# Adapter probabilities and values appended to each head's own 64 keys: transposes of 74 columns and value matmuls of 74 rows in four column tiles

## The chip, the cores and the metric

The kernel runs on one core of one Trainium2 chip. The metric is the device time of one execution in microseconds (us); lower is better. The time before is the median of three runs.

## What is computed

Two layers on `x` of shape (32, 64, 1024), kept in float32:

1. `x = x + attn(cond(x))`: a conditioned 64x64 mixing of channels, then causal self-attention with 32 heads of width 32, rotary angles, and an adapter: 10 learned prefix tokens whose keys and values come from the same weights.
2. `x = x + ffn(cond2(x))`: a grouped convolution, a 1024x1024 linear layer and a routed low-rank addition.

The change is in the attention only. The lines that matter there:

```python
attn = softmax(where(causal, q @ k.T / sqrt(hd), -inf))     # 64 keys per sequence
y = attn @ v
ascores = gating[0] * softmax(q @ ak.T / sqrt(C))           # 10 adapter keys, a softmax of its own
y = y + ascores @ av
out = y @ w_proj
```

The two softmaxes are separate, but both products end in the same `y`.

## The kernel before

Engines are programmed by hand, each with its own list of instructions and semaphores. The attention is 8 groups of 4 heads (`g`, 128 channels each) times 4 units of 512 tokens (`u`): 32 units `n = 4 g + u`. A unit has 8 sequences of 64 tokens, that is 4 pairs `s` of two (`b`).

On TensorE a unit (`unit_step`, L977) runs in this order: scores of the unit before (L900, four row tiles by two column tiles, one bank `bS[h]` for each head, a slot of 74 columns: 64 own keys and 10 adapter keys), transposes of its values (L960), projection of K (24 matmuls, L948), of Q (24), in a group's first unit the adapter's keys and values (`project_adapter`, L972, 16 starts in four column tiles), then the transposes of the probabilities of the unit before (`attend_transposes`, L906), projection of V (24), and last the value matmuls of the unit before (`attend_values`, L920). In a group's first unit `turn_adapter` (L936) stands in the middle of V. After unit 31 the same steps stand between the first products of the projection layer.

The softmax of a unit is on VectorE (`attend_softmax`, L1382) with exponentials on ScalarE (`attend_exp`, L1173). The own probabilities lie in `prob[t]`, two heads in each half of the columns, so that one transpose turns 2 x 64 columns. The adapter probabilities are weighted by the gate, split into a high part, a low part and the high part again (L1425 to L1428), and written as 3 x 40 columns of `aprob`; four transposes turn them (L909). ScalarE copies the turned banks back (`attend_copies`, L1180: `aT` and two `pT`). The adapter's product is then one reduced-precision matmul per unit over all four heads, with a block-diagonal `avbd` that VectorE prepares per group from two parts (L1648 to L1653); the own products add to it, with a block-diagonal `vbd` for two heads at once:

```python
pe.matmul(y[:], avbd[:], aT[:], start=True, stop=True)                               # L925
for s, b, hp:                                                                        # 16 matmuls
    pe.matmul(y[64*hp : 64*hp+64, cols], vbd[:, s, b, hp, :], pT[hp][:, s, 64*b:...]) # L931
```

A float32 matmul that is not a transpose appears in the trace as two starts, so L931 has 32 in a unit and L900 64. ScalarE fills `vbd` with four copies (L1291). SP stores the finished `y` and moves the prepared weights of the second layer (`store_prep`, L691) and, in a group's last unit, the next group's weights `w_st` (L754); `split_hi` (L1165) on ScalarE waits for these. After the attention come eight groups of projection products (L1026) and eight of the second layer (convolution L1044, products L1026, low rank L1078).

Of the kernel before, what the change touches and what calls it, by code (L numbers as in the profile page):

```python
# [32 lines left out]
P = 128  # L33
# [348 lines left out]
def program(nc, d, psum, z, zbase, y_dram, x1_dram, w_forms, ctx_dram, aggb_dram, weights, out):  # L382
# [8 lines left out]
    with ExitStack() as ctx:  # L391
# [64 lines left out]
        aprob = sb("aprob", [P, UP, P], F32R)  # L456
        atmp = sb("atmp", [P, UP * GH, NA])
        astat = sb("astat", [P, 3, UP * GH])
        aT = sb("aT", [P, UT], F32R)
        akv = sb("akv", [AC * AP_, 2 * P])  # L460
        avbd = sb("avbd", [P, P], F32R)
        avs = sb("avs", [P, P])
        avh = sb("avh", [P, P], F32R)
        asel = sb("asel", [AC * AP_, P])
        afold = sb("afold", [AC * AP_, NA])
        alow = sb("alow", [P, 1])
        amask = sb("amask", [P, P])
# [24 lines left out]
        bAT, bPT, bAD = bS[0], bS[1:3], bS[3]  # L492
        score_slots = psum[:, 0:GH * UP * SW].rearrange("p (h s c) -> p h s c", h=GH, c=SW)
        AKT, AVS = 2 * P, 3 * P
        AR = GH * NA
# [29 lines left out]
        agated = sem("a_agated")  # L525
        aprobs = sem("a_aprobs")
        a_tr = sem("a_a_tr")
        aT_copied = sem("a_aT_copied")
# [3 lines left out]
        avh_set = sem("a_avh_set")  # L532
        aweighted = sem("a_aweighted")
        aprob_hi = sem("a_aprob_hi")
# [6 lines left out]
        NCONST, NCLEAR, NFCONST = 10, 3, 3  # L541
# [48 lines left out]
        def place(t):  # L590
# [7 lines left out]
            (place(kbd_pad), place(qr), place(bbase), [place(t) for t in (x8[0], prob[0], pT[0], vbd)],  # L598
             [place(t) for t in (vT, aprob, aT, ysb)], attn.at))
        mix_sync, mix_clear, mix_tensor, mix_scalar, mix_vector = parts  # L600

        block = ctx.enter_context(nc.Block())

# [6 lines left out]
        def refill(g, u):  # L610

            return u == NU - 1 and not last(g)

# [46 lines left out]
        def _(sp):  # L660
            mix_sync.begin(sp)
            for dst, src in ((wte[:, 0:KC * NA], "wteT"), (cosT[:], "cos"), (sinT[:], "sin"), (mask[:], "mask"), (ident[:], "ident"),
                             (gate[:], "gate"), (asel[:], "asel"), (amask[:], "amask"), (afold[:], "afold"), (alow[:], "alow")):
                sp.dma_start(dst, d[src]).then_inc(consts, 16)
# [190 lines left out]
        def _(pool):  # L855
            mix_clear(pool)
            pool.memset(wte[:, KC * NA:], 0.0).then_inc(cleared, 1)
            pool.wait_ge(z_sum, 2 * UP)
            pool.memset(aprob[:].bitcast(F32), 0.0).then_inc(cleared, 1)
            pool.wait_ge(z_mm, NP)  # L860
            pool.memset(vbd[:], 0.0).then_inc(cleared, 1)
# [23 lines left out]
        def _(pe):  # L885
            mix_tensor.begin(pe)
            def attend_scores(m, groups):
# [48 lines left out]
            def turn_adapter(g):  # L936
                pe.wait_ge(akv_copied, g + 1)
                pe.matmul(bAD[:, AVS:AVS + P], asel[:], akv[:, P:2 * P], start=True, stop=True)
                pe.matmul(bAD[:, AKT:AKT + NA], akv[:, 0:P], afold[:], start=True, stop=True).then_inc(ak_tr, 1)
# [23 lines left out]
            def project_adapter(g, n):  # L963
# [5 lines left out]
                wait(pe, ashifted, n)  # L969
                for c in range(KC):  # L970
                    part = c % AP_
                    mm = pe.matmul(bAD[AC * part:AC * (part + 1), 0:2 * P], wte[:, c * NA:c * NA + AC],  # L972
# [141 lines left out]
            pe.wait_ge(ashifted, NG * NU)  # L1114
# [39 lines left out]
        def _(act):  # L1154
# [18 lines left out]
            def attend_exp(m):  # L1173
                for t in range(2):
                    act.wait_ge(shifted, 2 * m + t + 1)
                    act.activation(prob[t][:], prob[t][:], ACT.Exp, scale=SCALE).then_inc(exped, 1)  # L1176
                act.wait_ge(ashifted, m + 1)
                act.activation(atmp[:], atmp[:], ACT.Exp, scale=ASCALE).then_inc(aexped, 1)
# [65 lines left out]
            def unit_step(g, u):  # L1244
# [42 lines left out]
                if n == 0:  # L1287
                    act.wait_ge(cleared, NCLEAR)
# [561 lines left out]
```

## Time and profile before

| | |
|---|---|
| median of 3 runs | 1140.98 us (1140.66 to 1142.0) |
| span of the profiled execution, first to last instruction | 1139.1 us |
| its own time as a run | not listed apart; the median lies 1.9 us above its span |
| TensorE busy | 1132.2 us, 99% |
| VectorE busy | 923.4 us, 81% |
| ScalarE busy | 359.6 us, 32% |
| GpSimd busy | 54.1 us, 5% |
| granted TensorE clock, mean over the span | 1.000 |

In the profile a matmul's duration reaches from its start to the modelled end of its result, so matmuls in a row overlap; what one costs is read from start to start. Rows of the timeline merge instructions of one kind that follow each other: a start, the length of the whole piece, and their count.

### The profile page before, as it was taken

To read this page: it belongs to the slowest core of one execution; us is meant where nothing else is said; L and a number is where in the kernel's file an instruction comes from. 1 tells how busy PE (TensorE), PEld (TensorE's weight loads), DVE (VectorE), ACT (ScalarE), POOL (GpSimd) and SP (SyncE) were. 2 spreads that over 40 slices of the span, in tenths; PEclk is the share of its full clock that TensorE was granted. 3 is DMA by queue.
4 is the path that set the end of the run, shared out by engine and by line. 5 is a ranking of instruction groups with operands and counts; after the bars stand their busy time and mean duration, and the time that the engine had idled before them with its cause. 6 is when DMAs were issued, how large, how long until landed. Compare 5 with 4: busy or idle time off the path is not lost.

```text
span 1139.1 us, 21477 instructions
## 1 busy us (share of the span) xinstructions
PE 1132.2 (99%) x8632; PEld 950.7 (83%) x8632; DVE 923.4 (81%) x1740; ACT 359.6 (32%) x665; POOL 54.1 (5%) x24
## 2 busy tenths in 40 slices
PE   9999999999999999999999999999999999999998
PEld 6888888888888888888888888878888888888887
DVE  5999879879889789798798799888767777877765
ACT  5433333333342432433433334323222211122210
POOL 0000000000000000000000000110000022221112
PEclk9999999999999999999999999999999999999999
DMA  6515115114125034034033177885549933233312
GB/s 222 182 56 167 67 34 162 66 53 153 56 75 167 20 97 155 12 106 146 20 111 130 45 270 269 322 251 164 185 129 347 345 89 104 96 116 116 98 38 93
DMA packets 99701, 151.81 MB, mean 133 GB/s; under 512 B 7443, under 2 KB 84115, under 8 KB 96915
## 3 DMA queue, kind: packets, MB, share of 16 engines
q1 hardware_dynamic: 98594, 135.76, 36.5%
q10 hardware_dynamic: 1008, 14.68, 3.1%
q8 instruction: 69, 1.13, 0.4%
q14 instruction: 30, 0.24, 0.1%
HBM read 95.88 MB, written 54.54 MB: 132 GB/s over the span
## 4 chain that ended last, share of the span: by engine, by line
PE 92%; DVE 4%; DMA 2%; issue 1%; ACT 0%; SPq 0%; DVEq 0%; ACTq 0%
PE psum L948 44%; PE psum L1026 23%; PE psum L1044 5%; PE psum L931 3%; PE psum L916 2%; PE psum L900 2%; PE psum L1078 2%; PE psum L1060 2%; PE psum L276 2%; DMA y_scratch<-a_ysb 2%; PE psum L960 2%; PE psum L909 1%; PE psum L1062 1%; PE psum L972 1%; PE psum L230 1%
## 5 line engine op out<-in xcount | busy, mean ns | idle before, releaser
L948 PE MATMUL psum<-z,w_hi 128*128 128x512 f32 x1536 | 481.5, 395 | 0.2 <-DVE z L374 0.2
L948 PEld LDWEIGHTS psum<-z,w_hi 128*128 128x128 f32 x1536 | 282.5, 188 | 57.2 <-DVE z L374 0.4
L948 PE MATMUL psum<-z,w_lo 128*128 128x512 f32 x768 | 300.5, 391 | 0.0
L1026 PE MATMUL psum<-f_wform,f_act_hi 128*128 128x512 f32 (+1 forms) x912 | 279.9, 389 | 1.3 <-DVE f_u L1494 1.1
L1026 PEld LDWEIGHTS psum<-f_wform,f_act_hi 128*128 128x128 f32 x912 | 167.9, 188 | 35.8 <-issue 2.6
L1026 PE MATMUL psum<-f_wform,f_act_lo 128*128 128x512 f32 (+1 forms) x456 | 176.2, 386 | 0.0
L948 PEld LDWEIGHTS psum<-z,w_lo 128*128 128x128 f32 x768 | 144.1, 188 | 30.6
L1026 PEld LDWEIGHTS psum<-f_wform,f_act_lo 128*128 128x128 f32 x456 | 85.7, 188 | 17.4
L875 POOL TENSOR_TENSOR f_xn<-f_x,_bbase 128x1024 f32<-128x1024 f32 x16 | 50.5, 3158 | 1009.0 <-DVE f_x L1520 678.5
L1218 ACT ACTIVATE f_act_hi<-f_act_sum 128x512 fp32r<-128x512 f32 x64 | 40.3, 632 | 119.2 <-DVE f_act_sum L1469 48.1
L1218 ACT ACTIVATE f_act_hi<-f_raw 128x512 fp32r<-128x512 f32 x56 | 33.7, 626 | 102.7 <-DVE f_raw L1552 64.8
L1394 DVE TENSOR_TENSOR a_prob<-psum,a_mask 128x512 f32<-128x512 f32 x64 | 43.9, 687 | 26.4 <-PE psum L900 26.3
L1475 DVE TENSOR_TENSOR f_act_lo<-f_act_sum,f_act_hi 128x512 fp32r<-128x512 f32 x64 | 48.6, 762 | 16.5 <-ACT f_act_hi L1218 16.5
L1475 DVE TENSOR_TENSOR f_act_lo<-f_raw,f_act_hi 128x512 fp32r<-128x512 f32 x56 | 37.2, 689 | 28.6 <-ACT f_act_hi L1218 28.5
L1183 ACT ACTIVATE a_aT<-psum 128x512 fp32r<-128x512 f32 x32 | 19.2, 599 | 122.0 <-PE psum L909 121.8
L1291 ACT ACTIVATE a_vbd<-psum 64x256 f32<-64x256 f32 x128 | 48.5, 379 | 26.3 <-PE psum L960 25.1
L1176 ACT ACTIVATE a_prob<-a_prob 128x512 f32<-128x512 f32 x64 | 40.5, 633 | 51.4 <-DVE a_prob L1399 50.9
L1372 DVE STREAM_SHUFFLE a_rot<-psum 128x512 f32<-128x512 f32 x64 | 47.2, 737 | 0.0
L1411 DVE TENSOR_TENSOR a_prob<-a_prob,a_stat 128x512 f32<-128x512 f32 x64 | 44.3, 692 | 2.2
L1375 DVE TENSOR_TENSOR a_rot<-a_rot,a_sin 128x512 f32<-128x512 f32 x64 | 44.3, 692 | 2.2
L1399 DVE TENSOR_TENSOR a_prob<-a_prob,a_stat 128x512 f32<-128x512 f32 x64 | 44.3, 692 | 2.2
L1397 DVE TENSOR_REDUCE a_stat<-a_prob 128x8 f32<-128x512 f32 x64 | 44.0, 687 | 2.2
(173 smaller groups left out, 1491.7 us busy)
## 6 DMA issues: line engine op xcount, KB each, us to landing
w_forms<-f_prep_lo SPq DMA_DIRECT2D x16, 896.0 KB, 5.2
f_wform<-w_forms SPq DMA_DIRECT2D x7, 2048.0 KB, 13.2
f_wform<-w_forms ACTq DMA_DIRECT2D x7, 2048.0 KB, 16.9
w_st<-in_wqkvT SPq DMA_DIRECT2D x7, 1536.0 KB, 6.3
w_forms<-f_prep_hi SPq DMA_DIRECT2D x16, 640.0 KB, 6.2
m_x<-in_x SPq DMA_DIRECT2D x16, 512.0 KB, 5.5
y_scratch<-a_ysb SPq DMA_DIRECT2D x32, 256.0 KB, 2.8
f_raw<-y_scratch SPq DMA_DIRECT2D x8, 1024.0 KB, 6.0
```

What stands on the lines that cost most here:

```text
L875: pool.tensor_tensor(xn[:, t, :].rearrange("p (m q) -> p q m", q=PH), x1[:, t, :].rearrange("p (q m) -> p q m", q=PH), bbase[:].rearrange( ...
L948: mm = pe.matmul(dst, w[:, c, x, :], zs, start=(c == 0 and i == 0), stop=(c == KC - 1 and i == 2))
L1026: mm = pe.matmul((prod_bank[i], bank[0])[part][:, cols], a[:, c, :], wform[i][:, w, c, cols], start=(i < 4 and c == 0 and n == 0), stop=(c ...
L1044: mm = pe.matmul(conv_banks(p)[:, o:o + P], x8[p % 2][:, CONV * b + g, j:j + P], toep[:, g, j, :], start=(j == 0), stop=(j == 1))
L1218: act.activation(act_hi[f][:], src, ACT.Copy).then_inc(act_hi_set, 1)
L1291: cp = act.activation(vbd[NC * h:NC * (h + 1), :, b, :, HD * h:HD * (h + 1)], bV[NC * b:NC * (b + 1), :].rearrange("p (s a h e) -> p s a h ...
L1372: dve.stream_shuffle(rot[:], src[:], HALF_SWAP).then_inc(turned[x], 1)
L1375: dve.tensor_tensor(r, r, tab[1], ALU.mult).then_inc(rot_step, 1)
L1397: dve.tensor_reduce(stat[:, t, 0, :], prob[t][:], AX, ALU.max).then_inc(row_max, 1)
L1399: dve.tensor_tensor(prob[t][:], prob[t][:], spread(t, 0), ALU.subtract).then_inc(shifted, 1)
L1411: dve.tensor_tensor(prob[t][:], prob[t][:], spread(t, 2), ALU.mult).then_inc(probs, 1)
L1475: dve.tensor_tensor(act_lo[f][:], src, act_hi[f][:].bitcast(F32), ALU.subtract).then_inc(act_set, 1)
```

## The change

Each head gets its own strip of 74 columns in `prob`, 64 own probabilities and behind them its 10 adapter probabilities. A transpose turns 128 tokens x 74 columns (16 in a unit, into the four score banks), ScalarE copies 74 rows four times, and the value matmul of a head has 74 rows: the keys' values (`vkeys`, rows 0 to 63) and the adapter's values times the gate (rows 64 to 73, copied per group from `avt`). The four heads go to four column tiles of 32. The separate adapter matmul, its split into parts, `aprob`, `aT`, `avbd`, `avs`, `avh`, two constants (`amask`, `alow`, two DMAs on SP's queue) and two clearing writes on GpSimd are gone. From group 1 on the adapter's projection stands in the bank of `y` and no longer in `bS[3]`.

```diff
-        vbd = sb("vbd", [P, UP, 2, 2, 2 * HD])
-        prob = [sb(f"prob{t}", [P, 8, NC]) for t in range(2)]
-        pT = [sb(f"pT{t}", [P, UP, P]) for t in range(2)]
+        vkeys = sb("vkeys", [P, UP, 2, P])
+        prob = sb("prob", [P, GH, UP, KW])
+        pT = sb("pT", [P, GH, UT])
...
             def attend_scores(m, groups):
-                wait(pe, aT_copied, m)
-                wait(pe, pT_copied, 2 * m)
-                wait(pe, ashifted, m)
+                wait(pe, pT_copied, GH * m)
...
             def attend_transposes(m):
-                pe.wait_ge(aprobs, 2 * m + 2)
-                for i in range(UP):
-                    tr = pe.transpose(bAT[:, i * P:(i + 1) * P], aprob[:, i, :].bitcast(F32),
-                                      ident[:])
-                tr.then_inc(a_tr, 1)
-                wait(pe, pT_copied, 2 * m)
-                for t, dst in enumerate(bPT):
-                    pe.wait_ge(probs, 2 * m + t + 1)
-                    for j in range(4):
-                        tr = pe.transpose(dst[:, j * P:(j + 1) * P],
-                                          prob[t][:, 2 * j:2 * j + 2, :].rearrange("p h k -> p (h k)"), ident[:])
+                pe.wait_ge(aprobs, m + 1)
+                for h in range(GH):
+                    pe.wait_ge(probs, 2 * m + h // 2 + 1)
+                    for s in range(UP):
+                        tr = pe.transpose(bS[h][0:KW, s * P:(s + 1) * P], prob[:, h, s, :], ident[:])
                     tr.then_inc(p_tr, 1)
 
             def attend_values(m, groups):
                 y = y_bank(m)
-                pe.wait_ge(aT_copied, m + 1)
+                turns = min((m + 1) // NU + 1, NG)
+                pe.wait_ge(akbd_set, turns)
+                pe.wait_ge(avs_set, turns)
                 pe.wait_ge(avbd_set, groups)
                 wait(pe, y_copied, m)
-                pe.matmul(y[:], avbd[:], aT[:], start=True, stop=True)
                 pe.wait_ge(vbd_set, m + 1)
-                pe.wait_ge(pT_copied, 2 * m + 2)
+                pe.wait_ge(pT_copied, GH * (m + 1))
                 for s in range(UP):
                     for b in range(2):
-                        for hp in range(2):
-                            mm = pe.matmul(y[2 * HD * hp:2 * HD * (hp + 1), (2 * s + b) * NC:(2 * s + b + 1) * NC],
-                                           vbd[:, s, b, hp, :], pT[hp][:, s, NC * b:NC * b + NC],
-                                           start=False, stop=True, skip_group_check=True)
+                        for h in range(GH):
+                            rows = slice(HD * h, HD * (h + 1))
+                            cols = slice((2 * s + b) * NC, (2 * s + b + 1) * NC)
+                            mm = pe.matmul(y[rows, cols], vkeys[0:KW, s, b, rows], pT[0:KW, h, cols], start=True, stop=True)
...
             def attend_copies(m):
-                act.wait_ge(a_tr, m + 1)
                 wait(act, y_mm, m)
-                act.activation(aT[:], bAT[:], ACT.Copy).then_inc(aT_copied, 1)
-                for t, src in enumerate(bPT):
-                    act.wait_ge(p_tr, 2 * m + t + 1)
-                    act.activation(pT[t][:].rearrange("p s q -> p (s q)"), src[:], ACT.Copy).then_inc(pT_copied, 1)
+                if m == 0:
+                    act.wait_ge(z_sum, 3 * UP)
+                for h in range(GH):
+                    act.wait_ge(p_tr, GH * m + h + 1)
+                    act.activation(pT[0:KW, h, :], bS[h][0:KW, :], ACT.Copy).then_inc(pT_copied, 1)
...
-                dve.tensor_scalar(astat[:, 2, :], astat[:, 2, :], gate[:, 0:1], None, ALU.mult).then_inc(agated, 1)
-                dve.tensor_tensor(atmp[:], atmp[:], aspread(2), ALU.mult).then_inc(aweighted, 1)
-                dve.tensor_copy(parts[:, 0], flat).then_inc(aprob_hi, 1)
-                dve.tensor_tensor(parts[:, 1], flat, parts[:, 0].bitcast(F32), ALU.subtract).then_inc(aprobs, 1)
-                dve.tensor_copy(parts[:, 2], parts[:, 0].bitcast(F32)).then_inc(aprobs, 1)
+                dve.tensor_tensor(prefix, prefix, aspread(2), ALU.mult).then_inc(aprobs, 1)
```

Three places in the order of the instructions. First, TensorE between the end of Q's projection (`z`, `w_hi`, `w_lo`: activations and weights in parts) and V's, in the second unit; `_ident` is the moving identity. Before, and then with the change:

```order
L948 MATMUL psum<-z,w_hi 128x512 x2
L948 MATMUL psum<-z,w_lo 128x512
L909 MATMUL psum<-_ident,a_aprob 128x128 x4
L916 MATMUL psum<-_ident,a_prob_107 128x128 x4
L916 MATMUL psum<-_ident,a_prob_108 128x128 x4
```

```order
L931 MATMUL psum<-z,w_hi 128x512 x2
L931 MATMUL psum<-z,w_lo 128x512
L898 MATMUL psum<-_ident,a_prob 74x128 x16
L931 MATMUL psum<-z,w_hi 128x512 x2
L931 MATMUL psum<-z,w_lo 128x512
```

Twelve transposes of 128x128 have become sixteen of 74x128; line numbers moved with the file (L948 is now L931).

Second, TensorE behind V's projection, where the value matmuls stand. Before (the pair of `a_pT` rows comes eight times in all), and then with the change:

```order
L948 MATMUL psum<-z,w_hi 128x512 x2
L948 MATMUL psum<-z,w_lo 128x512
L925 MATMUL psum<-a_aT,a_avbd 128x512
L931 MATMUL psum<-a_pT_109,a_vbd 64x64
L931 MATMUL psum<-a_pT_110,a_vbd 64x64
```

```order
L931 MATMUL psum<-z,w_hi 128x512 x2
L931 MATMUL psum<-z,w_lo 128x512
L915 MATMUL psum<-a_pT,a_vkeys 32x64 x32
L887 MATMUL psum<-a_kbd,a_qr 64x74 x32
L943 MATMUL psum<-_ident,a_vT 128x128 x4
```

The matmul of 512 columns is gone, sixteen matmuls of 64x64 have become thirty-two of 32x64, and scores (now L887) and value transposes (now L943) follow as they did.

Third, VectorE at the end of a softmax, where the adapter's part stands ahead of the rotation of K (`a_kr`). Before, and then with the change:

```order
L1413 TENSOR_REDUCE a_astat<-a_atmp 128x16
L1415 RECIPROCAL a_astat<-a_astat 128x16
L1417 TENSOR_SCALAR a_astat<-a_astat,a_gate 128x16
L1420 TENSOR_TENSOR a_atmp<-a_atmp,a_astat 128x160
L1425 CAST a_aprob<-a_atmp 128x4x4x10
L1427 TENSOR_TENSOR a_aprob<-a_atmp,a_aprob 128x4x4x10
L1428 CAST a_aprob<-a_aprob 128x4x4x10
L1370 TENSOR_TENSOR a_kr<-psum,a_cos 128x512
```

```order
L1392 TENSOR_TENSOR a_prob<-a_prob,a_stat 128x8x64
L1394 TENSOR_REDUCE a_astat<-a_prob 128x16
L1396 RECIPROCAL a_astat<-a_astat 128x16
L1398 TENSOR_TENSOR a_prob<-a_prob,a_astat 128x16x10
L1352 TENSOR_TENSOR a_kr<-psum,a_cos 128x512
```

Four of the seven adapter steps are gone, and the rotation of K follows the weighting directly.

## Rows read from the trace of the kernel before

**Rows 1.** The page: busy time and share of each engine, and TensorE's granted clock by slices.

```profile
PE 1132.2 (99%) x8632; PEld 950.7 (83%) x8632; DVE 923.4 (81%) x1740; ACT 359.6 (32%) x665; POOL 54.1 (5%) x24
...
PEclk9999999999999999999999999999999999999999
```

**Rows 2.** Waits of TensorE, longest of eight: us in total, times, longest.

```profile
PE psum L230 <- DVE m_busy L319: 1.5, 1, 1.5
```

**Rows 3.** Timeline of TensorE, one unit: start us, us, line, tiles, shapes, count.

```profile
327.87 0.60 PE L909 MATMUL psum<-_ident,a_aprob 128*128 128x128 f32 x4
328.31 1.04 PE L916 MATMUL psum<-_ident,a_prob 128*128 128x128 f32 x8
329.10 0.71 PE L948 MATMUL psum<-z,w_hi 128*128 128x512 f32 x2
...
334.44 0.39 PE L948 MATMUL psum<-z,w_lo 128*128 128x512 f32 x1
334.67 0.39 PE L925 MATMUL psum<-a_aT,a_avbd 128*128 128x512 f32 x1
334.99 1.15 PE L931 MATMUL psum<-a_pT,a_vbd 128*64 128x64 f32 x32
336.07 0.94 PE L900 MATMUL psum<-a_kbd,a_qr 32*64 32x74 f32 x64
336.94 0.66 PE L960 MATMUL psum<-_ident,a_vT 128*128 128x128 f32 x4
```

**Rows 4.** Groups of TensorE weight loads by form: busy us, mean ns.

```profile
L1044 PEld LDWEIGHTS psum<-_toep,_x 128*128 128x128 f32 x256 | 29.3, 192 | 0.1
L916 PEld LDWEIGHTS psum<-_ident,a_prob 128*128 128x128 f32 x256 | 28.9, 140 | 0.0
```

**Rows 5.** Groups of TensorE matmuls by form: busy us, mean ns.

```profile
L1044 PE MATMUL psum<-_toep,_x 128*128 128x128 f32 x256 | 29.9, 275 | 0.0
L972 PE MATMUL psum<-w_st,a_wte 128*32 128x256 f32 x128 | 8.6, 385 | 0.0
```

**Rows 6.** Timeline of TensorE at the adapter's projection in a group's first unit.

```profile
305.81 1.07 PE L972 MATMUL psum<-w_st,a_wte 128*32 128x256 f32 x16
306.81 0.66 PE L909 MATMUL psum<-_ident,a_aprob 128*128 128x128 f32 x4
```

**Rows 7.** Timeline of VectorE at the end of a softmax, same unit as rows 3.

```profile
324.96 0.23 DVE L1417 TENSOR_SCALAR a_astat<-a_astat,a_gate 128x16 f32<-128x16 f32 x1
325.23 0.32 DVE L1420 TENSOR_TENSOR a_atmp<-a_atmp,a_astat 128x160 f32<-128x160 f32 x1
325.59 0.24 DVE L1425 CAST a_aprob<-a_atmp 128x160 fp32r<-128x160 f32 x1
...
326.12 0.23 DVE L1428 CAST a_aprob<-a_aprob 128x160 fp32r<-128x160 f32 x1
```

**Rows 8.** Timeline of ScalarE in the last unit of group 1.

```profile
205.87 1.06 ACT L1171 ACTIVATE w_hi<-w_st 128x1024 fp32r<-128x1024 f32 x1 [10.57 <-DMA w_st<-in_wqkvT]
206.95 0.60 ACT L1183 ACTIVATE a_aT<-psum 128x512 fp32r<-128x512 f32 x1
207.45 1.08 ACT L1186 ACTIVATE a_pT<-psum 128x512 f32<-128x512 f32 x2
208.40 1.07 ACT L1171 ACTIVATE w_hi<-w_st 128x1024 fp32r<-128x1024 f32 x1
```

**Rows 9.** Timeline of TensorE in the same unit.

```profile
208.29 0.39 PE L925 MATMUL psum<-a_aT,a_avbd 128*128 128x512 f32 x1
208.68 1.15 PE L931 MATMUL psum<-a_pT,a_vbd 128*64 128x64 f32 x32
```

**Rows 10.** Waits of SP's queue, that for the second layer's stored weights.

```profile
SPq L753 <- DMA w_forms<-a_prep_hi_two: 30.7, 7, 4.7
```

**Rows 11.** Timeline of VectorE in group 3's first unit.

```profile
311.76 0.29 DVE L1648 TENSOR_TENSOR a_avs<-psum,a_amask 128x128 f32<-128x128 f32 x1 [1.23 <-ACT a_kbd L1267]
```

**Rows 12.** Timeline of TensorE in the same unit.

```profile
314.17 0.39 PE L925 MATMUL psum<-a_aT,a_avbd 128*128 128x512 f32 x1
```

More of the change, by code:

```diff
@@ L540, in program @@
         y_out = sem("a_y_out")
-        NCONST, NCLEAR, NFCONST = 10, 3, 3
+        NCONST, NFCONST = 8, 3
         fconsts = sem("f_consts")
@@ L597, in program, with own @@
             (wst, whi, wlo, whi_f, w_first, w_hi, w_lo),
-            (place(kbd_pad), place(qr), place(bbase), [place(t) for t in (x8[0], prob[0], pT[0], vbd)],
-             [place(t) for t in (vT, aprob, aT, ysb)], attn.at))
+            (place(kbd_pad), place(qr), place(bbase), [place(t) for t in (x8[0], prob, pT, vkeys)],
+             [place(vT), place(pT) + 2 * UT * 4, place(pT) + 3 * UT * 4, place(ysb)], attn.at))
         mix_sync, mix_clear, mix_tensor, mix_scalar, mix_vector = parts
         block = ctx.enter_context(nc.Block())
+        prefix = prob[:].rearrange("p h s c -> p (h s) c")[:, :, NC:KW]
+        def own(t):
+            return prob[:, 2 * t:2 * t + 2, :, 0:NC].rearrange("p h s k -> p (h s) k")
         def first(g, u):
@@ L612, in refill, with adapter_bank @@
             return u == NU - 1 and not last(g)
+        def adapter_bank(g):
+            return bY if g else bS[3]
         def y_bank(m):
@@ L968, in project_adapter @@
                 pe.wait_ge(w_lo[V_], g + 1)
-                wait(pe, ashifted, n)
+                wait(pe, y_copied, n - 1)
                 for c in range(KC):
                     part = c % AP_
-                    mm = pe.matmul(bAD[AC * part:AC * (part + 1), 0:2 * P], wte[:, c * NA:c * NA + AC],
+                    mm = pe.matmul(adapter_bank(g)[AC * part:AC * (part + 1), 0:2 * P], wte[:, c * NA:c * NA + AC],
                                    wst[:, c, K_:V_ + 1, :].rearrange("p x c -> p (x c)"),
@@ L1286, in unit_step @@
                 wait(act, y_mm, n)
-                if n == 0:
-                    act.wait_ge(cleared, NCLEAR)
-                for b in range(2):
-                    for h in range(2):
-                        cp = act.activation(
-                            vbd[NC * h:NC * (h + 1), :, b, :, HD * h:HD * (h + 1)],
-                            bV[NC * b:NC * (b + 1), :].rearrange("p (s a h e) -> p s a h e", s=UP, a=2, h=2)[:, :, :, h, :],
-                            ACT.Copy)
+                if u == 0:
+                    act.wait_ge(avs_set, g + 1)
+                    act.activation(vkeys[NC:KW, :, :, :].rearrange("p s b f -> p (s b) f"),
+                                   avt[NC:KW, :].rearrange("p (a f) -> p a f", a=1).broadcast_to([NA, UB, P]),
+                                   ACT.Copy).then_inc(avbd_set, 1)
+                for b in range(2):
+                    cp = act.activation(vkeys[0:NC, :, b, :], bV[NC * b:NC * (b + 1), :].rearrange("p (s f) -> p s f", s=UP),
+                                        ACT.Copy)
                 cp.then_inc(vbd_set, 1)
@@ L1392, in attend_softmax @@
                     dve.wait_ge(scores, 2 * m + t + 1)
-                    wait(dve, p_tr, 2 * m)
-                    dve.tensor_tensor(prob[t][:].rearrange("p (s h) k -> p h s k", h=2),
-                                      score_slots[:, 2 * t:2 * t + 2, :, 0:NC], maskb, ALU.add).then_inc(masked, 1)
+                    wait(dve, p_tr, GH * m)
+                    dve.tensor_tensor(prob[:, 2 * t:2 * t + 2, :, 0:NC], score_slots[:, 2 * t:2 * t + 2, :, 0:NC], maskb, ALU.add
+                                      ).then_inc(masked, 1)
                     dve.wait_ge(masked, 2 * m + t + 1)
-                    dve.tensor_reduce(stat[:, t, 0, :], prob[t][:], AX, ALU.max).then_inc(row_max, 1)
+                    dve.tensor_reduce(stat[:, t, 0, :], own(t), AX, ALU.max).then_inc(row_max, 1)
                     dve.wait_ge(row_max, 2 * m + t + 1)
-                    dve.tensor_tensor(prob[t][:], prob[t][:], spread(t, 0), ALU.subtract).then_inc(shifted, 1)
+                    dve.tensor_tensor(own(t), own(t), spread(t, 0), ALU.subtract).then_inc(shifted, 1)
                 asrc = score_slots.rearrange("p h s c -> p (h s) c")[:, :, NC:KW]
@@ L1402, in attend_softmax @@
                 dve.wait_ge(amax, m + 1)
-                wait(dve, aprobs, 2 * m)
-                dve.tensor_tensor(atmp[:], asrc, aspread(0), ALU.subtract).then_inc(ashifted, 1)
+                dve.tensor_tensor(prefix, asrc, aspread(0), ALU.subtract).then_inc(ashifted, 1)
                 for t in range(2):
                     dve.wait_ge(exped, 2 * m + t + 1)
-                    dve.tensor_reduce(stat[:, t, 1, :], prob[t][:], AX, ALU.add).then_inc(row_sum, 1)
+                    dve.tensor_reduce(stat[:, t, 1, :], own(t), AX, ALU.add).then_inc(row_sum, 1)
                     dve.wait_ge(row_sum, 2 * m + t + 1)
@@ L1410, in attend_softmax @@
                     dve.wait_ge(inverted, 2 * m + t + 1)
-                    dve.tensor_tensor(prob[t][:], prob[t][:], spread(t, 2), ALU.mult).then_inc(probs, 1)
+                    dve.tensor_tensor(own(t), own(t), spread(t, 2), ALU.mult).then_inc(probs, 1)
                 dve.wait_ge(aexped, m + 1)
-                dve.tensor_reduce(astat[:, 1, :], atmp[:], AX, ALU.add).then_inc(asum, 1)
+                dve.tensor_reduce(astat[:, 1, :], prefix, AX, ALU.add).then_inc(asum, 1)
                 dve.wait_ge(asum, m + 1)
@@ L1647, in unit_step @@
                     wait(dve, avbd_set, g)
[L1648 to L1653 removed]
+                    dve.tensor_scalar(avt[NC:KW, :], adapter_bank(g)[NC:KW, AVS:AVS + P], gate[NC:KW, 0:1], None, ALU.mult
+                                      ).then_inc(avs_set, 1)
                 if n == 0:
@@ L1783, in constants @@
     q, k = np.arange(P)[:, None] % NC, np.arange(NC)[None, :]
-    row, part = np.arange(P) % (GH * NA), np.arange(P) // (GH * NA)
     kv = np.arange(AC * AP_) % AC
     return {
-        "asel": ((row[None, :] % NA == kv[:, None]) & (part < 3)[None, :]).astype(np.float32),
+        "asel": ((kv[:, None] < NA) & (np.arange(P)[None, :] - NC == kv[:, None])).astype(np.float32),
         "afold": (kv[:, None] == np.arange(NA)[None, :]).astype(np.float32),
-        "alow": (part == 2)[:, None].astype(np.float32),
-        "amask": ((row[:, None] // NA == np.arange(P)[None, :] // HD) & (part < 3)[:, None]).astype(np.float32),
         "cos": np.tile(np.concatenate([cos, cos], 0), (GH, 1)),
```

51 lines of the change are left out of this document (9 added, 42 removed).

## The prediction

> **What bounds the kernel now.** First the page [rows 1]: TensorE is busy 1132.2 of 1139.1 us, 99%, and its clock is granted in full in all forty slices. VectorE stands at 81%, ScalarE at 32%. A busy TensorE need not be a bound, since durations overlap, so the next view is the list of its waits: there are eight in the whole span, the longest 1.5 us at the very start, before the attention [rows 2]. In the attention TensorE waits for nobody. So an instruction that it is given more, or spared, moves the end by its own start-to-start cost, and what VectorE or ScalarE save is worth nothing by itself. The third view is therefore TensorE's timeline of one unit [rows 3], where costs are read as the distance from one start to the next. All that the change does to the time is in two places of that unit, 32 times.
>
> **Transposes: 12 become 16.** Four transposes take 328.31 - 327.87 = 0.44 us, 0.11 us each [rows 3]. The question is what that price hangs on, because a transpose now has 74 columns in its stationary operand and still streams the 128 columns of the identity. The rows let the two be told apart: the load of a transpose takes 140 ns and that of a full float32 matmul 192 ns [rows 4], yet a 128-column float32 start of the convolution has nearly the same busy time per start, 29.9 us over 256 starts or 0.117 us [rows 5], as the transposes' 0.11. A load shorter by 52 ns bought almost nothing. I take the streamed 128 columns as the price, unchanged: 16 x 0.11 instead of 12 x 0.11, +0.44 us a unit. The other end, a price that falls with the columns, is the first rival.
>
> **The adapter's own matmul goes.** From the last start of V at 334.44 to L925 at 334.67 is 0.23 us, and L925 is an ordinary 512-column start in that row of starts [rows 3]. Without it the value matmuls follow V directly; the change of tiling in front of them stands either way. So -0.23 us a unit.
>
> **Value matmuls: 32 starts in two column tiles become 64 in four.** Before, the block takes 336.07 - 334.99 = 1.08 us [rows 3]. No row shows the new form, so I bound it. What a streamed column costs: 385 ns for 256 columns against 275 ns for 128 [rows 5], 110 ns per 128, so 0.055 us for 64. With two tiles at once 32 starts are 16 rounds, 0.88 us, and 0.20 us of the 1.08 are entry, exit and loads. With four tiles at once 64 starts are again 16 rounds, 0.88 us. That four tiles of 128 rows by 32 columns do run at once is what the adapter's projection shows: 16 starts of 256 columns take 306.81 - 305.81 = 1.00 us [rows 6]; four at once is 4 x 0.22 = 0.88 us plus 0.12, two at once would be 1.76. So the block is 1.00 us if its remainder is the projection's 0.12, and 1.08 if it is the old block's 0.20. A high bound comes from charging the projection's 0.12 us in full to its four rounds, 0.03 a round: 16 x 0.085 = 1.36 us. The old block, with 16 rounds as well, is the nearest row and contradicts that (0.20 in 16 rounds), so I take 1.05, -0.03 us a unit; 1.00 and 1.36 stay as ends.
>
> **ScalarE.** Three copies of turned banks become four. In the tightest place they run 207.45 - 206.95 = 0.50 us apart [rows 8], so the last ends 0.5 us later, beside V's projection (334.44 - 329.10 = 5.3 us [rows 3]). Only in the last unit of a group is that cover thin, because the copies stand behind a weight copy that waited 10.57 us for the DMA [rows 8]; in group 1 they end at 207.45 + 1.08 = 208.53 and the value matmuls start at 208.68 [rows 9]. If that cover went, 0.5 us less the 0.18 us by which the values start later would be exposed, 0.3 us, in seven units at most: 2 us. But it should widen: VectorE's adapter tail loses 325.23 - 324.96 = 0.27 us and 326.12 + 0.23 - 325.59 = 0.76 us, some 1.0 us [rows 7]; the prepared weights that VectorE makes in a group's third unit are then stored earlier, and SP waits for that store (seven times, up to 4.7 us [rows 10]) before it asks for the next weights. The four copies into `vbd` become two of twice the size, and per group ten rows are copied once more; ScalarE has room for both.
>
> **VectorE, SP, GpSimd.** The softmax ends 1.0 us earlier than 326.35 and the transposes it feeds start at 327.87 [rows 3, 7]: slack becomes more slack. In a group's first unit the values now also wait for the adapter's values, set at 311.76 + 0.29 = 312.05 [rows 11]; L925 stood at 314.17 there [rows 12], so 2 us are left. SP's queue has two constants fewer to send in the first stage and GpSimd two clears fewer; nothing that TensorE waits for is among them, so zero.
>
> **The sum.** +0.44 - 0.23 - 0.03 = +0.18 us a unit, 32 units, +5.8 us. Against the profiled execution: span 1139.1 becomes 1144.9; the median of the runs lies 1.9 us above that span and I leave that distance, so 1141.0 + 5.8 = **1146.8 us**, 0.5% slower. With the low end of the block: +0.13 a unit, +4.2, 1145.2. With the high end: +0.49 a unit, +15.7, 1156.7, of little weight for the reason given.
>
> **Rival 1, faster: the transpose's price follows its 74 columns.** Place: the 16 transposes of a unit. If a start cost 74/128 of 0.11, 0.064 us, they would take 1.02 instead of 1.32 us, and the unit 0.30 + 0.23 + 0.03 = 0.56 us less: -17.9 us, 1123.1. The point at which it decides is a price of (1.32 + 0.26)/16 = 0.099 us: below it the kernel gets faster. For it: the stationary operand really is narrower. Against it: the comparison of loads above [rows 4, 5]. I give 0.06 to a clear gain and another 0.06 to a price near 0.099, which would be no change. The Trainium skill, "TensorE: Matmul & The Clock Gate", section "LDWEIGHTS (loading the stationary operand)", says that a load's time goes by its columns, 1/1.2 ns each; by that rule the loads of 74 columns get shorter, and this rival follows if loads set the pace. The rows show that transposes' loads are not what sets it.
>
> **Rival 2, much slower: only two tiles at once.** If 64 starts ran in pairs, the block would be 32 x 0.055 + 0.20 = 1.96 us, +0.88: the unit +1.09, +34.9 us, 1175.9. Against it: the projection's 1.00 us [rows 6]. What could still part the two is 74 rows instead of 128. Chance 0.04.
>
> **Rival 3, much slower: a price per start.** The old block spends 1.08/32 = 0.034 us on a start; 64 starts at that price are 2.16 us, +1.08, the unit +1.29, +41.3 us, 1182.3. Against it stand the scores, 64 starts in 336.94 - 336.07 = 0.87 us, 0.0136 each [rows 3], and the new block needs only 0.0164. Chance 0.04. The Trainium skill has such a rule on the same page, in the section "Wait — 56ns, not 53.3ns?": starts never come closer than about 25 ns, however few columns. By it the block would take at least 64 x 0.025 = 1.6 us, an estimate of 1164 us for the run; this trace's scores disagree with it by almost a factor of two, since they run on several tiles.
>
> **Rival 4, a little more: thin covers.** The late copies above are exposed after all, or the scores behind the longer block start with fewer instructions ready. Up to 2 us for the first; the second I bound by 0.05 us a unit, the difference between 1.05 and the block's 1.00, 1.6 us. That is 1147 to 1150.4, the same sign. Chance 0.08.
>
> **How the numbers follow.** The forecast gets 0.72, and with rival 4 the band from 1145.2 to 1150.4 holds 0.80. The low end of the range goes a step towards rival 1, to a transpose of 0.105 us: 16 x 0.105 - 1.32 - 0.26 = +0.10 us a unit, +3.2, 1144.2. The high end stays at 1150.4. About 0.2%, or 2.3 us, is what a measurement of this kernel tells from no change: under 1138.7 faster, above 1143.3 slower. Faster 0.06 (rival 1), same 0.06, slower 0.88 (0.72 + 0.08 + 0.04 + 0.04).
>
> **What would show it.** Right: sixteen transposes whose starts stay 0.11 us apart, about 1.75 us to V's first start; V's last start followed directly by the value matmuls; 64 of these in 1.0 to 1.1 us up to the first score; the scores' 0.87 us kept; no new waits of TensorE. Wrong: transposes closer than 0.10 us (rival 1); starts of value matmuls coming two at a time, or evenly 0.03 us apart (rivals 2 and 3); waits of the value matmuls for `a_pT` in each group's last unit (rival 4). If the time fell while TensorE's timeline showed these costs, the claim that nothing else bounds the kernel would be wrong.

## The result, and the profile after

| | before | after |
|---|---|---|
| median of 7 runs each, us | 1142.0 (1140.66 to 1144.9) | 1148.02 (1144.92 to 1152.8) |
| ratio of the times | | 1.0059, 95% interval [1.0047, 1.0071] |
| span of the profiled execution, us | 1139.1 | 1143.1 |

The changed kernel is slower by 0.6%, about 6 us. Its profiled execution took 1144.92 us, the fastest of its seven runs; why will be seen below. The page after, busy time of each engine and granted clock, against [rows 1]:

```profile
PE 1134.9 (99%) x9752; PEld 954.4 (83%) x9752; DVE 891.9 (78%) x1596; ACT 372.0 (33%) x641; POOL 52.8 (5%) x22
...
PEclk9999999999999999999999999999999999999999
```

VectorE lost 31.5 us of work and TensorE won nothing by it. VectorE's timeline shows where the softmax now ends:

```profile
325.80 0.33 DVE L1398 TENSOR_TENSOR a_prob<-a_prob,a_astat 128x160 f32<-128x160 f32 x1
```

It ends at 326.13 and the transposes start at 328.72, 2.59 us later, where 1.52 us lay between them before [rows 3, 7]: slack became more slack. TensorE's timeline of the unit that [rows 3] show (start us, us, line, tiles, shapes, count):

```profile
328.49 0.39 PE L931 MATMUL psum<-z,w_lo 128*128 128x512 f32 x1
328.72 1.91 PE L898 MATMUL psum<-_ident,a_prob 128*74 128x128 f32 x16
330.38 0.71 PE L931 MATMUL psum<-z,w_hi 128*128 128x512 f32 x2
...
335.72 0.39 PE L931 MATMUL psum<-z,w_lo 128*128 128x512 f32 x1
336.04 1.10 PE L915 MATMUL psum<-a_pT,a_vkeys 74*32 74x64 f32 x64
337.07 0.94 PE L887 MATMUL psum<-a_kbd,a_qr 32*64 32x74 f32 x64
337.95 0.66 PE L943 MATMUL psum<-_ident,a_vT 128*128 128x128 f32 x4
```

Read from start to start:

| step of a unit, us | before [rows 3] | after | difference |
|---|---|---|---|
| transposes, to V's first start | 329.10 - 327.87 = 1.23 | 330.38 - 328.72 = 1.66 | +0.43 |
| V's last start to the first value matmul | 334.99 - 334.44 = 0.55 | 336.04 - 335.72 = 0.32 | -0.23 |
| value matmuls, to the first score | 336.07 - 334.99 = 1.08 | 337.07 - 336.04 = 1.03 | -0.05 |
| scores, to the transposes of the values | 0.87 | 0.88 | +0.01 |

That is +0.16 us a unit. The view of one line gives the first and last start of its instructions; the scores' line spans units 0 to 31, so 31 units from first to last (fields after the count: shortest, median and longest ns, then first to last start). Before, after, and the changed kernel profiled a second time:

```profile
L900 PE MATMUL psum<-a_kbd,a_qr x2048: 222/223/273, 64.1 to 712.4; 32*64 32x74 f32 x187
```

```profile
L887 PE MATMUL psum<-a_kbd,a_qr x2048: 222/223/273, 62.1 to 716.3; 32*64 32x74 f32 x187
```

```profile
L887 PE MATMUL psum<-a_kbd,a_qr x2048: 222/223/274, 68.4 to 722.0; 32*64 32x74 f32 x187
```

The attention takes 648.3 us before, 654.2 and 653.6 after: +5.9 and +5.3, of which 31 units of +0.16 are 5.0. The stage ahead of it ends at 64.1, 62.1 and 68.4; over the thirteen profiles of this case it ends at 63.8 to 68.3 in the kernel before and its variants and at 62.1 to 68.4 in the changed one and its. Of the 7.5 us between the two profiled runs of the changed kernel (1144.92 and 1152.39) this stage makes 6.3. The stretch from the last score to the end varies less, 426.4 to 428.3 and 426.8 to 428.8 us. So in what follows the attention is read from this row, and the run's time beside it.

What the prediction had not settled was the late copies. TensorE's waits after (us in total, times, longest):

```profile
PE psum L230 <- DVE m_busy L319: 1.4, 1, 1.4
PE psum L915 <- ACT a_pT L1168: 1.0, 2, 0.6
```

The second row is new [rows 2]: in two units the value matmuls wait for ScalarE's copies. Both are last units of a group. ScalarE and TensorE in the first of them, group 0 (in brackets: idle before, and what ended it):

```profile
120.58 1.06 ACT L1153 ACTIVATE w_hi<-w_st 128x1024 fp32r<-128x1024 f32 x1 [10.78 <-DMA w_st<-in_wqkvT]
121.66 2.04 ACT L1168 ACTIVATE a_pT<-psum 74x512 f32<-74x512 f32 x4
```

```profile
123.01 0.39 PE L931 MATMUL psum<-z,w_lo 128*128 128x512 f32 x1
123.85 1.10 PE L915 MATMUL psum<-a_pT,a_vkeys 74*32 74x64 f32 x64 [0.45 <-ACT a_pT L1168]
```

The four copies take 2.04 us where three took 208.53 - 206.95 = 1.58 [rows 8], and they start when the weight copy ahead of them has its DMA. The cover did not widen. SP's queue tells why: in that unit before, then after.

```profile
106.29 0.37 SPq L676 DMA_DIRECT2D y_scratch<-a_ysb  x1
106.70 0.51 SPq L696 DMA_DIRECT2D w_forms<-f_prep_lo  x1
...
110.21 0.59 SPq L696 DMA_DIRECT2D w_forms<-a_prep_hi_two  x1
115.28 0.35 SPq L754 DMA_DIRECT2D w_st<-in_wqkvT  x1
```

```profile
104.45 0.36 SPq L669 DMA_DIRECT2D y_scratch<-a_ysb  x1
104.86 1.65 SPq L689 DMA_DIRECT2D w_forms<-f_prep_lo  x1
...
107.17 1.26 SPq L689 DMA_DIRECT2D w_forms<-a_prep_hi_two  x1
113.00 0.34 SPq L747 DMA_DIRECT2D w_st<-in_wqkvT  x1
```

The stores of the prepared weights stand behind the store of `y` in that queue and begin 0.41 us after it in both kernels, so the chain starts with TensorE's value matmuls, whose `y` ScalarE copies for that store, and not with VectorE. From the store of `y` to the request for `w_st` it takes 7.9 to 9.0 us in the seven groups before and 8.2 to 9.5 after. From that request to ScalarE's copy of the landed weights it takes 6.25 to 6.90 us before and 6.55 to 7.58 after, 0.4 more in the mean; why is not shown. So the copies, which in the seven groups before ended 0.15 to 1.72 us ahead of the value matmuls, now end 0.5 to 0.9 ahead in five groups and hold them up in two.

### The profile page after: what moved, and what is told of

The parts are those of the page before. It is cut to its first block, busy times and chain, and to the rows that moved or that the text cites. A ratio compares the mean times of both kernels' runs of the same rounds, so it can differ in the third digit from the quotient of the medians.

```text
span 1143.1 us, 23476 instructions
## 1 busy us (share of the span) xinstructions
PE 1134.9 (99%) x9752; PEld 954.4 (83%) x9752; DVE 891.9 (78%) x1596; ACT 372.0 (33%) x641; POOL 52.8 (5%) x22
## 4 chain that ended last, share of the span: by engine, by line
PE 91%; DMA 5%; DVE 2%; issue 1%; ACT 1%; SPq 0%; DVEq 0%; ACTq 0%
PE psum L931 42%; PE psum L1009 24%; PE psum L1027 5%; PE psum L898 4%; PE psum L915 3%; PE psum L887 2%; PE psum L1061 2%; PE psum L1043 2%; PE psum L276 2%; DMA y_scratch<-a_ysb 2%; PE psum L943 1%; DMA w_st<-in_wqkvT 1%; DMA w_forms<-a_prep_hi_two 1%; PE psum L1045 1%; PE psum L955 1%
## 5 line engine op out<-in xcount | busy, mean ns | idle before, releaser
L931 PE MATMUL psum<-z,w_hi 128*128 128x512 f32 x1536 | 482.1, 395 | 0.0
L931 PEld LDWEIGHTS psum<-z,w_hi 128*128 128x128 f32 x1536 | 282.5, 188 | 56.5 <-issue 0.4
L931 PE MATMUL psum<-z,w_lo 128*128 128x512 f32 x768 | 300.1, 391 | 0.0
L931 PEld LDWEIGHTS psum<-z,w_lo 128*128 128x128 f32 x768 | 144.1, 188 | 31.4
L1168 ACT ACTIVATE a_pT<-psum 74x512 f32<-74x512 f32 x128 | 65.4, 591 | 124.2 <-PE psum L898 124.0
L898 PE MATMUL psum<-_ident,a_prob 128*74 128x128 f32 x512 | 61.3, 273 | 0.0
L898 PEld LDWEIGHTS psum<-_ident,a_prob 128*74 128x74 f32 x512 | 55.7, 116 | 6.6 <-issue 2.9
L1341 DVE TENSOR_TENSOR w_lo<-w_st,w_hi 128x1024 fp32r<-128x1024 f32 x21 | 25.7, 1225 | 27.2 <-ACT w_hi L1153 27.2
```

What stands on the lines that cost most here:

```text
L898: tr = pe.transpose(bS[h][0:KW, s * P:(s + 1) * P], prob[:, h, s, :], ident[:])
L931: mm = pe.matmul(dst, w[:, c, x, :], zs, start=(c == 0 and i == 0), stop=(c == KC - 1 and i == 2))
L1168: act.activation(pT[0:KW, h, :], bS[h][0:KW, :], ACT.Copy).then_inc(pT_copied, 1)
```

## The experiments

All ratios are against the kernel before, run beside it on the same chip; its medians there were 1141.06 to 1141.28 us.

**The changed kernel again.** No edit.

> The changed kernel once more, beside the two that follow, so that they share a chip. Theory: the end moves by TensorE's own starts, 20.50 us a unit becomes 20.67 us, +5.3 us over 32 units, and on top of it come waits of the value matmuls for late copies in some groups' last units, 1.0 us in the profile at hand: 1146 to 1149 us against 1141 to 1142 before, units of 20.67 us again. Rival (the difference is a matter of the first stage and of chance): the ratio falls to 1.002 or less.

1148.38 us (1148.09 to 1152.39), ratio 1.006 [1.0046, 1.0074]; its profile is the second one above, with one wait for `a_pT` of 0.5 us. The slowdown is settled, and so is that the short profiled execution of the first run owes its time mainly to its first stage, 62.1 against 68.4 us.

**Copies ahead of the weight copy.** In a group's last unit ScalarE does the copies of the turned banks first; the same edit in both kernels (shown for the one before, L1248 to L1262).

```diff
                     attend_exp(n - 1)
-                if refill(g, u):
-                    split_hi(K_, g + 1, n + 1)
                 if n == 0:
...
                 if refill(g, u):
+                    split_hi(K_, g + 1, n + 1)
                     split_hi(Q_, g + 1, n + 1)
```

> In a group's last unit ScalarE makes the four copies of transposed probabilities ahead of the copy of K's next weights, which waits for a DMA. Theory (the values wait for copies that stand behind that DMA): no wait of the value matmuls for a_pT is left, every last unit takes 20.67 us, 1 to 2 us less than the changed kernel, about 1146. Rival (those waits only move to the next weights or elsewhere, or do not count): the same time within 0.5 us and a new wait of similar size.

> The same exchange in the kernel before, whose copies ended only 0.14 to 1.7 us ahead of the value matmuls in the last units. Theory: in most executions nothing waited there, so no change within 0.1%; if some executions have late DMAs, the upper ones of its times (up to 1144.9) get rarer, up to 1 us off the median. Rival (the exchange itself costs, because K's next weights come later): slower by 0.5 us or more.

The changed kernel: 1147.8 us, ratio 1.0053 [1.0039, 1.0067]; no wait for `a_pT` is left. The gain is 0.6 us where I expected 1 to 2. The kernel before: 1141.18 us, 0.9997 [0.9985, 1.001], its attention 648.2 us, so the exchange by itself costs nothing. The scores of the first:

```profile
L887 PE MATMUL psum<-a_kbd,a_qr x2048: 222/223/273, 64.9 to 718.0; 32*64 32x74 f32 x187
```

653.1 us of attention, 1.1 less than in the first profile after and 0.5 less than in the second: just the waits that went. So rival 4's late copies cost 0.5 to 1 us in these two profiles, and the rest, 4.8 us over the kernel before, lies in the units themselves. The time of this run is 6.7 us over the kernel before; the 1.9 us beyond the attention stand outside it and are no more than the stages there vary by.

**Value matmuls two tiles at a time.** Heads 0 and 1 first, then 2 and 3: the same 64 starts, but only two neighbouring column tiles at once.

```diff
-                for s in range(UP):
+                for hh in range(2):
+                  for s in range(UP):
                     for b in range(2):
-                        for h in range(GH):
+                        for h in (2 * hh, 2 * hh + 1):
```

> The 32 value matmuls of a unit in another order: first all of heads 0 and 1, then all of heads 2 and 3, so that only two column tiles can run at once. Theory (the block is rounds of tiles that run at once, 16 rounds of 0.056 us): 32 rounds, the block grows from 1.03 to 1.9 to 2.0 us, +28 to +31 us in all, 1175 to 1179. Rival (a price per start, whatever the tiles): block and time unchanged, 1.03 us and about 1148.

1169.11 us, a single run. TensorE's timeline of a unit:

```profile
345.93 1.79 PE L916 MATMUL psum<-a_pT,a_vkeys 74*32 74x64 f32 x64
347.66 0.94 PE L887 MATMUL psum<-a_kbd,a_qr 32*64 32x74 f32 x64
```

The block takes 1.73 us instead of 1.03 with the same starts, so a price per start (rival 3) is refuted and the four tiles do run at once. The size was less than expected, 1.9 to 2.0. Inside the block the mean distance of starts is 0.025 us with two tiles and 0.014 with four. The single starts of the trace say why. With four tiles four starts come within 0.02 us and then the next four, in sixteen rounds that begin 0.056 us apart (0.080 behind the first). With two tiles two come 0.006 us apart, and the next two again after 0.056 us (346.070, 346.126, 346.182); but where the order passes to heads 2 and 3, between 346.63 and 346.84, rounds of both pairs run side by side, and from the first start to the last the block has about 28 lengths of a round in place of 31. So a round costs the same with two tiles as with four, and what I had wrong was their number.

**The price of a transpose, and of the adapter's matmul.** The adapter's four transposes twice, 16 in all; and, apart from it, the adapter's matmul left out, so that `y` lacks the adapter's share.

```diff
-                for i in range(UP):
+                for i in [*range(UP), *range(UP)]:
                     tr = pe.transpose(bAT[:, i * P:(i + 1) * P], aprob[:, i, :].bitcast(F32),
```

```diff
-                pe.matmul(y[:], avbd[:], aT[:], start=True, stop=True)
...
-                                           start=False, stop=True, skip_group_check=True)
+                                           start=True, stop=True)
```

> The kernel before with its four adapter transposes made twice, sixteen in a unit instead of twelve. Theory (each transposes costs its streamed 128 columns, 0.109 us, and nothing hides it): units of 20.94 us instead of 20.50, +14.0 us, 1155. Rival (part of a unit's starts lies beside other work): clearly less than +14.

> The kernel before without the 512-column adapter matmul; the adapter's share is left out of y. Theory: 0.227 us a unit, units of 20.27 us, -7.3 us, 1133.8. Rival (the matmul partly covers the change of tiling that follows it): 0.10 to 0.15 us a unit, -3 to -5 us.

The first: 1156.38 us, ratio 1.0133 [1.0119, 1.0148]. The second: 1136.55 us, 0.9957 [0.994, 0.9974]. Their scores, in this order:

```profile
L900 PE MATMUL psum<-a_kbd,a_qr x2048: 222/223/274, 68.3 to 729.3; 32*64 32x74 f32 x187
```

```profile
L900 PE MATMUL psum<-a_kbd,a_qr x2048: 222/223/274, 68.2 to 709.4; 32*64 32x74 f32 x187
```

Four more transposes of 128 columns make the attention 661.0 us, +12.7 or 0.41 a unit over 31 units, against the change's +0.43 for four more of 74: the columns of the stationary operand do not show. Without the matmul it is 641.2 us, -7.1 or 0.23 a unit, the term of the sum to the digit. The median of that run fell by 4.5 us only; two of its four executions took 1134.05 and 1134.85 us, and the profiled one, at 1138.25, had a first stage that ended at 68.2 where the kernel before has 64.1. The first stages of the others are not on record.

**Adapter transposes in float32r.** The kernel before, its adapter probabilities (already rounded) turned as 120 columns against a rounded copy of the identity.

```diff
-                    tr = pe.transpose(bAT[:, i * P:(i + 1) * P], aprob[:, i, :].bitcast(F32),
-                                      ident[:])
+                    tr = pe.transpose(bAT[0:3 * AR, i * P:(i + 1) * P].bitcast(F32R), aprob[:, i, 0:3 * AR],
+                                      identr[:])
```

The adapter's matmul and the copy ahead of it then run over 120 rows, and one clearing write on GpSimd is gone.

> The kernel before with its four adapter transposes in float32r (the adapter's probabilities are already split into such parts, so the values stay what they were; the identity gets a copy in that type; 120 instead of 128 columns are turned). Theory (the price of a transpose is the streaming of the 128 columns, two clocks of TensorE a column in float32 and one in float32r): 0.055 to 0.065 us instead of 0.109, -0.18 to -0.22 us a unit, -6 to -7 us, about 1134.5, faster than both kernels. Rival (the load of the stationary columns then sets the pace, as in the convolution's 0.111): unchanged within 1 us.

1137.42 us, ratio 0.997 [0.9958, 0.9981]: faster than both kernels, though the gain is 3.6 us where I expected 6 to 7. Its timeline, and its weight loads of this form:

```profile
329.15 0.44 PE L910 MATMUL psum<-a_identr,a_aprob 128*120 128x128 f32 x4
329.43 1.06 PE L917 MATMUL psum<-_ident,a_prob 128*128 128x128 f32 x8
...
330.25 0.71 PE L949 MATMUL psum<-z,w_hi 128*128 128x512 f32 x2
```

```profile
L910 PEld LDWEIGHTS psum<-a_identr,a_aprob 128*120 128x120 f32 x128 | 13.5, 136 | 6.2 <-issue 2.9
```

Four transposes take 0.28 us instead of 0.44, though a load takes nearly as long, 136 ns against 140 [rows 4]; the float32 transposes behind them take 0.82 instead of 0.79 and give some of it back. So the price hangs on the type of the transpose. Both operands changed type; since the load hardly did in time, I put it down to the streaming of the 128 columns.

**Two constants still loaded.** The changed kernel with `amask` and `alow` in SP's queue as before, unused.

```diff
-        NCONST, NFCONST = 8, 3
+        NCONST, NFCONST = 10, 3
...
-                             (gate[:], "gate"), (asel[:], "asel"), (afold[:], "afold")):
+                             (gate[:], "gate"), (asel[:], "asel"), (amask[:], "amask"), (afold[:], "afold"), (alow[:], "alow")):
```

> The changed kernel with the two constants that it no longer needs still loaded, so that SP's queue in the first stage is that of the kernel before. Theory (the first stage does not care): 1147 to 1148.5, as the changed kernel. Rival (about 1 us of the measured 6.7 comes from the first stage, whose DMAs now stand otherwise): about 1147 or less, and the first scores at 64.1 us again, where profiles of the changed kernel had them at 62.1, 68.4 and 64.9.

1146.92 us (1146.31 to 1150.9), ratio 1.0059 [1.0047, 1.0071], the changed kernel's own ratio; the attention takes 653.2 us, with one wait for `a_pT` of 0.2 us, and the first score comes at 65.1. Those two transfers don't make the slowdown. A share of about 1 us, the rival, is not excluded: the time lies at the border of the two expectations, and a first score at 65.1 is inside what the stage varies by anyway.

**All transposes of the probabilities in float32r, in both kernels.** The last multiplications of the softmax write rounded probabilities into a tile of their own, so these versions compute less precisely than the two kernels. The kernel before takes over the 120-column form of its adapter transposes. For the changed kernel:

```diff
+        probr = sb("probr", [P, GH, UP, KW], F32R)
+        identr = sb("identr", [P, P], F32R)
...
-                        tr = pe.transpose(bS[h][0:KW, s * P:(s + 1) * P], prob[:, h, s, :], ident[:])
+                        tr = pe.transpose(bS[h][0:KW, s * P:(s + 1) * P].bitcast(F32R), probr[:, h, s, :], identr[:])
...
-                    dve.tensor_tensor(own(t), own(t), spread(t, 2), ALU.mult).then_inc(probs, 1)
+                    dve.tensor_tensor(own_r(t), own(t), spread(t, 2), ALU.mult).then_inc(probs, 1)
...
-                dve.tensor_tensor(prefix, prefix, aspread(2), ALU.mult).then_inc(aprobs, 1)
+                dve.tensor_tensor(prefix_r, prefix, aspread(2), ALU.mult).then_inc(aprobs, 1)
```

> All sixteen transposes of a unit in float32r: the last softmax multiplications write rounded probabilities into a tile of their own, and the identity is a rounded copy (the probabilities are rounded to float32r, so the output's precision changes). My theory, transposes pay for streamed identity columns and float32r streams them faster: at the 0.067 us a start and the 0.077 us to the next instruction that the adapter's transposes took, the block takes 15 x 0.067 + 0.077 = 1.08 us instead of 1.66, with some 0.04 us given back by V's entry and others, -0.54 us a unit, about 1130 us, faster than the kernel before by 1%. Rival, the price of a 74-column transpose is a floor of its own that float32 does not set: block still above 1.4 us and a time above 1138.

> The kernel before with its twelve transposes in float32r in the same way (its own probabilities are rounded as well). My theory: 11 x 0.067 + 0.077 = 0.81 us instead of 1.23, 0.03 us given back, -0.39 us a unit, about 1128.5 us. Against the changed kernel at the same transpose price the difference is then 4 x 0.067 - 0.23 - 0.05 = -0.01 us a unit, so the two must stand within 2 us of each other: the change is worth nothing, and costs only what float32 transposes cost. Rival, the change costs something beside its transposes: the changed kernel stays 4 us or more behind this one.

The changed kernel: 1128.69 us, ratio 0.9891 [0.9875, 0.9908]. The kernel before: 1133.21 us, 0.9928 [0.9912, 0.9945]. Their timelines, changed kernel first:

```profile
323.22 1.14 PE L907 MATMUL psum<-a_identr,a_probr 128*74 128x128 f32 x16
324.20 0.67 PE L940 MATMUL psum<-z,w_hi 128*128 128x512 f32 x2
```

```profile
324.33 0.44 PE L911 MATMUL psum<-a_identr,a_aprob 128*120 128x128 f32 x4
324.61 0.85 PE L918 MATMUL psum<-a_identr,a_probr 128*128 128x128 f32 x8
325.29 0.69 PE L950 MATMUL psum<-z,w_hi 128*128 128x512 f32 x2
```

Sixteen transposes of 74 columns take 0.98 us, 0.061 each; eight of 128 columns take 0.68, 0.085 each; four of 120 columns 0.28, 0.070 each. The two kernels need nearly the same for their transposes (0.98 and 0.96). So what the change cost was the float32 price of its four more transposes: with that gone, the 0.23 and 0.05 us that it saves per unit stand alone. A plain unit takes 19.95 us against 20.24, the attention 633.6 against 640.3, and it is the faster kernel by 4.5 us, in spite of the late copies shown next. My expectation of a tie, at 1128.5 us for the kernel before, was wrong because I had charged 0.067 us to every form.

In float32r the form of the stationary operand does matter, and the single starts of these units show how. Loads of 74 columns start 0.062 us apart, of 120 columns 0.080, of 128 columns 0.086, and the transposes follow at that pace. Only the first three of 120 columns, the first of whose loads began 0.23 us ahead, follow each other after 0.058 and 0.062, so that 0.070 is a mean of two paces. So loads of 120 and 128 columns set the pace; with 74 columns the loads' pace is also the shortest one seen with 120, and which of the two sets it is not shown. In float32 the transposes start 0.109 us apart with 74 columns and with 128, more than any of these distances between loads. That the longer stream hides the loads there fits this, but no run takes the two apart in float32.

**The fastest version.** The float32r form of the changed kernel has shorter units, so its late copies show more:

```profile
PE psum L924 <- ACT a_pT L1177: 2.2, 3, 1.1
```

The last kernel adds the edit of the copies to it.

> The changed kernel with its sixteen transposes in float32r, and ScalarE's four copies of the turned banks ahead of K's weight copy in each group's last unit. In the float32r run alone the value matmuls waited 2.2 us in all for these copies, in three units, and the attention's units took 3.0 us more than 24 plain and 7 first ones. My theory, the late copies cost this: that wait gone, the 3.0 us fall below 1, about 1126 us. Rival, the order only moves the wait to K's weights: waits of the projections for the weight copies appear in its place and the time stays at 1128.7.

1125.26 us (1124.37 to 1127.72), ratio 0.9859 [0.9824, 0.9894]. The wait is gone, nothing took its place, and the scores run over 630.8 us, 17.5 less than in the kernel before:

```profile
L895 PE MATMUL psum<-a_kbd,a_qr x2048: 222/223/273, 64.1 to 694.9; 32*64 32x74 f32 x187
```

## Why the prediction was right, and where it was not

- **What bounds the kernel** was right: TensorE is at 99% as before, and the attention moved by what TensorE was given, 0.16 us a unit.
- **Transposes, +0.44 a unit**: +0.43. A transpose costs 1.66/16 = 0.104 us with 74 columns and 1.23/12 = 0.103 with 128 (0.109 from start to start in both blocks, and 0.03 from the last start to V's first), though the load did get shorter, as the groups of loads by form show against [rows 4]:

```profile
L898 PEld LDWEIGHTS psum<-_ident,a_prob 128*74 128x74 f32 x512 | 55.7, 116 | 6.6 <-issue 2.9
```

  It is 116 ns instead of 140. The prediction's comparison set a busy time per start of the convolution, 0.117, beside a start-to-start time, 0.11; from start to start the convolution has 0.111 with loads of 192 ns, so the conclusion stands. Rival 1 falls in float32: loads do not set the pace. The rule that the prediction quoted with it, from the Trainium skill, "TensorE: Matmul & The Clock Gate", section "LDWEIGHTS (loading the stationary operand)", agrees in direction, narrower is shorter; by its 1/1.2 ns a column 54 columns fewer would be an estimated 45 ns, and the rows show 24.
- **The adapter's matmul, -0.23**: -0.23 here, and by the run that left it out alone.
- **The value block, -0.03**: -0.05, 1.03 us inside the ends of 1.00 and 1.36; the tiles run four at once, as the starts in fours show, and the run with two shows the alternative at +0.70 us. Rivals 2 and 3 fall. Rival 3's rule, from the Trainium skill, the section "Wait — 56ns, not 53.3ns?" of the same page, would have asked for an estimated 1.6 us; 64 starts took 1.03, so here it does not hold across column tiles.
- **The scores' entry** (rival 4, second half): 0.88 against 0.87, nothing.
- **"But it should widen"** is a step that failed. I let the store of the prepared weights begin with VectorE's work; in SP's queue it stands behind the store of `y`, which waits for the value matmuls, and they are no earlier. The cover did not widen, the next weights even came some 0.4 us later after their request, and the copies grew by 0.46 us. So the late copies of rival 4, which had 0.08, came true in one or two of seven units: 1.0 and 0.5 us in the two profiles of the changed kernel, 0.2 in the one with the two constants, of the 2 us that bounded them.
- **The sum**: +0.18 a unit was +0.16, about 5.1 us for 32 units in place of 5.8, plus up to 1 us of late copies that the sum had at nothing. That these two errors nearly cancel is luck. The predicted 1146.8 us stands 1.2 us under the median of 1148.02, of which 1.0 is the kernel before itself: its median was 1140.98 when the prediction was made and 1142.0 beside the changed kernel. That rest lies within the interval of the ratio (0.0047 to 0.0071 of 1142.0, 5.4 to 8.1 us), and no run separates it.

## What to carry to other kernels

When the engine that bounds a kernel never waits, count what the edit gives that engine, start to start, in the unit that repeats; 31 us saved on VectorE were worth nothing here. Before merging work into more and narrower transposes, ask what a transpose is paid for: here it cost the same in float32 with 74 columns as with 128, and only after changing that price (float32r) did the merged form win. When a claim says that something starts earlier, follow its queue back to the instruction ahead of it, not to the engine that makes its data.

## What was not expected of the hardware

- Float32r transposes of the same 128 streamed columns take 0.061 us each (74 columns of stationary operand), 0.070 (120) and 0.085 (128) over their blocks, against 0.104 and 0.103 in float32 for 74 and 128. In float32r their starts go with those of the loads, 0.062, 0.080 and 0.086 us apart; in float32 both forms start 0.109 us apart.
- Float32 matmuls of 64 columns in rounds of two column tiles and of four start a new round after the same 0.056 us, so the tiles beyond two cost nothing in that block.
- The time to the first score, work that the change hardly touches, was 62.1 to 68.4 us from one profile to the next, more than the change is worth. A run's time alone could not have sized the terms of 0.05 to 0.2 us a unit; the start of the same line in units 0 and 31 could.
